# Three identity products between score products and row products in the gather loop of a graph-attention kernel

## The reference

```python
xn = _layernorm(x)
h = xn @ W_layer.T + b_layer
a1, a2 = h @ w_a1.T + b_a1, h @ w_a2.T + b_a2
v = leaky_relu(a1[row] + a2[col], 0.01)        # one score for each edge
ev = exp(v - segment_max(v, row)[row])
att = ev / segment_sum(ev, row)[row]
gnn = segment_sum(att[:, None] * h[col], row)  # the weighted rows, summed by target
x = x + gnn + mix(xn)                          # mix: the linear-attention branch
x = x + experts(_layernorm(x))                 # top 2 of 8, hidden width 682
```

## Time and profile before

| what | value |
|---|---|
| median of 3 runs | 2865.88 us |
| profiled execution | 2872.26 us |
| its span, first to last instruction | 2870.5 us |
| the gather, about | 440 to 1794 us of the span |
| PE busy, of the span | 2320.9 us (81%) |
| DVE busy, of the span | 1806.3 us (63%) |
| POOL busy, of the span | 1144.3 us (40%) |
| granted TensorE clock, mean of the span | 0.842 of full speed |

### The profile page before, as it was taken

One profiled execution on the slowest core, in us unless ns is written; L12 is line 12 of the kernel. 1 busy time (PEld: TensorE's weight loads), 2 busy tenths in 40 slices (PEclk: granted clock), 3 DMA queues, 4 the chain that ended last, 5 costly groups with the idle time before them and its releaser, 6 DMA issues.

```text
span 2870.5 us, 47292 instructions
## 1 busy us (share of the span) xinstructions
PE 2320.9 (81%) x12659; PEld 1906.3 (66%) x12683; DVE 1806.3 (63%) x6119; ACT 1253.3 (44%) x3758; POOL 1144.3 (40%) x1155
## 2 busy tenths in 40 slices
PE   3999984777877787778777878754599999999998
PEld 1677653555655565556555656643599999999997
DVE  8667763776777767777776667645355555555553
ACT  7444424555555555555555555432122222222222
POOL 0000005666666666666666663245222112112211
PEclk9999985788778777887788787765799999999999
DMA  2233213333333333333333335654122222222222
GB/s 71 92 115 99 90 59 85 88 89 89 89 89 89 89 89 89 89 88 89 90 89 89 89 88 52 213 179 157 52 36 36 34 36 35 36 34 36 36 35 28
DMA packets 127236, 226.62 MB, mean 79 GB/s; under 512 B 25553, under 2 KB 86482, under 8 KB 126214
## 3 DMA queue, kind: packets, MB, share of 16 engines
q0 software_dynamic: 62448, 142.98, 21.5%
q1 hardware_dynamic: 64534, 80.65, 9.0%
HBM read 169.81 MB, written 53.72 MB: 78 GB/s over the span
## 4 chain that ended last, share of the span: by engine, by line
PE 46%; DVE 18%; issue 16%; another core or an unknown queue 9%; DVEq 5%; POOL 2%; ACT 1%; DMA 1%; POOLq 0%; SPq 0%; ACTq 0%
PE psum L1614 18%; PE psum L1647 9%; PE psum L1102 6%; DVEq L1221 4%; DVE arena L1202 3%; PE psum L495 2%; DVE arena L824 2%; DVE arena L825 2%; DVE arena L1213 2%; PE psum L1353 1%; DVE arena L1246 1%; POOL expert_in L1574 1%; DVEq L1202 1%; PE psum L502 1%
## 5 line engine op out<-in xcount | busy, mean ns | idle before, releaser
L1075 POOL DMA_INDIRECT arena<-table,arena x880 | 864.2, 982 | 496.1 <-issue 235.9
L1102 PE MATMUL psum<-arena 128*128 128x257 f32 x1760 | 707.4, 540 | 293.6 <-DVE arena L1202 220.6
L1102 PEld LDWEIGHTS psum<-arena 128*128 128x128 f32 x1760 | 385.5, 255 | 509.3 <-issue 414.4
L1202 DVE SCALAR_TENSOR_TENSOR arena<-arena,psum 128x257 f32 x880 | 423.3, 481 | 358.8 <-remote 284.7
L1614 PE MATMUL psum<-arena 128*128 128x128 f32 x4620 | 552.1, 275 | 0.6 <-ACT arena L1669 0.6
L1614 PEld LDWEIGHTS psum<-arena 128*128 128x128 f32 x4620 | 542.5, 192 | 6.7 <-DVE arena L1711 0.9
L1751 POOL DMA_INDIRECT out<-arena x105 | 163.2, 1555 | 674.7 <-ACT arena L1676 664.6
L1129 ACT ACTIVATE arena<-arena 128x128 f32<-128x128 bf16 x880 | 281.2, 391 | 148.6 <-DVE arena L1216 108.4
L1647 PE MATMUL psum<-arena 128*128 x1260 | 290.5, 379 | 0.8 <-ACT arena L1676 0.8
L1142 ACT ACTIVATE arena<-arena 128x128 f32<-128x128 bf16 x880 | 281.2, 391 | 7.8 <-PE psum L1102 0.7
L1093 PEld LDWEIGHTS psum<-arena 128*128 128x128 f32 x1760 | 251.2, 220 | 19.1 <-issue 18.9
(11 more groups left out here) (332 smaller groups left out, 3093.1 us busy)
## 6 DMA issues: line engine op xcount, KB each, us to landing
arena<-table,arena POOLq DMA_INDIRECT x880
arena<-expert_in SPq DMA_DIRECT2D x105, 129.0 KB
mix_inputs<-arena SPq DMA_DIRECT2D x98, 128.0 KB
arena<-mix_inputs SPq DMA_DIRECT2D x49, 256.0 KB
arena<-in_w SPq DMA_DIRECT2D x6, 1364.0 KB
out<-arena SPq DMA_DIRECT2D x50, 128.0 KB
table<-arena SPq DMA_DIRECT2D x49, 129.0 KB
arena<-in_x SPq DMA_DIRECT2D x49, 128.0 KB, 3.6
```

The lines of the kernel that those rows point to most:

```text
L1075: pool.indirect_dma_start(rows_in[j][:, q * TW:(q + 1) * TW], None, table_d[:, :], bass.IndirectOffsetOnAxis(ap=col_all[:, t:t + 1], axis=0))\
L1102: mm(psum[4 + q][:, 0:C + 1], weight[b][:, q * P:(q + 1) * P], rows_in[g][:, q * TW:q * TW + C + 1], start=True, stop=True).then_inc(S("pr ...
L1202: v.scalar_tensor_tensor(here, here, alpha[(j - 5) % RING][:, q:q + 1], psum[4 + q][:, 0:C + 1], ALU.mult, ALU.add).then_inc(S("acc_done"), 1)
```

## The change

In each TensorE step that has score products, three more products are issued right behind the four score products and ahead of the four row products. Each multiplies the 128x128 identity matrix by itself, in float32, and writes 128 columns of PSUM bank i modulo 2. Nothing reads them: the transposes of the same step overwrite these columns. They carry no wait and no count, and `edge_done` is counted by the last score product, ahead of them.

```diff
@@ -53,6 +53,7 @@
 SLOPE = 0.01
+IDLE_GATHER = 3
 EPS = 1e-5
@@ -1093,6 +1094,8 @@
                         last = mm(psum[2 + b][:, 2 * q:2 * q + 2], member[b][:, q * P:(q + 1) * P], lb[b][:, q:q + G + 2:G + 1],
                                   start=True, stop=True)
                     last.then_inc(S("edge_done"), 1)
+                    for _ in range(IDLE_GATHER):
+                        mm(psum[b][:, 0:P], ident[:, :], ident[:, :], start=True, stop=True)
```

## The result

The change takes 2897.28 us (median of 4 runs, 2893.54 to 2899.50) beside 2863.07 us before (4 runs, 2858.85 to 2868.88): ratio 1.0117, 95% interval 1.0093 to 1.0140. It is slower by 34 us. The profiled execution of the change took 2895.72 us, its span is 2894.0 us, 23.5 us more than the span before.

What follows compares the result with a forecast made beforehand. The gather was taken as bound by waits on POOL's fetches, transfers and late-seen counts: 0 for 101 double steps, +2 for the end, 2865.9 + 2 = 2868 us; 2860 to 2876 if it holds, 8 in 10 for 2840 to 2905.

Steps and rivals of the forecast that it cites:

- TensorE as the bound at the lower clock: Slower rival, gather: low-clock double steps become TensorE-bound, 14.5 against 12.05 us; +15, +50 or +125 us; chance 0.27.
- What bounds the gather: Gather: a loop of POOL's eight fetches, their transfers and when product counts are seen sets 12.05 us, not TensorE's speed.
- double step: Gather: 12.05 us holding about two steps, eight POOL fetches and one wait each of POOL and DVE; 101 in 1217 us.
- The end of the gather: From 1775.45 us TensorE's own chain has no cover: two sets cost 1.4 to 2.6 us; taken as +2.
- The length of a set: Three added products in a gather step, six records: 0.72 us at the higher clock, 1.28 at the lower.
- The clock: Gather: denser TensorE work probably raises its granted clock somewhat; expected sign 0.78 or above.
- I cost this at nothing: Gather's 101 double steps: added TensorE work costs 0 us, covered by DVE's idle time and POOL's wait.
- The signs that the prediction named: Gather: 12.05 us double steps, 101 DVE waits of 2.8 us and POOL waits of 2.0 us, clock at least 0.78.
- Its last sign: The prediction fails if the late release of the counts in the gather hangs on TensorE's density; no size given.
- The faster rival: Gather: added products shift or break the late sight of counts; 10 to 30 us less, bound 2662 us; chance 0.19.

Runs made afterwards that it cites:

- free chip: Label for runs in which the kernel before takes 2594 to 2614 us; its profiled run there, without any edit, took 2608.15 us.
- held one: Held chip: label for runs in which the kernel before takes 2831 to 2869 us; the first measurement had 2863.07 us before.
- first chip: First measurement of the change, three products a step, against the kernel before: 2897.28 beside 2863.07 us, ratio 1.0117.
- second chip: Repeat of the unedited change against the kernel before, where that takes 2838.69 us: 2856.22 us, ratio 1.0058.
- e5_three: The change itself again, three products a step, no edit, against the kernel before: 2856.22 beside 2838.69 us, ratio 1.0058.
- e6_before_again: The kernel before, unedited, run once for its profile where the counts are not held back: 2608.15 us.

## Where the prediction was right and where it was wrong, point by point

The forecast was no change, 2868 us, and 2860 to 2876 us if its mechanism held; measured is 2897, +1.2%. That the time lies in the wide range of 2840 to 2905 us is luck: the range had been widened upward for TensorE as the bound at the lower clock, and that is not what came.

*What bounds the gather.* Right for the chip of the profile: the double step hangs on the fetches and on when counts are seen, and not on TensorE's speed. The free chip shows the same program without these waits. The prediction took the late counts for a property of the kernel; they depend on the chip or the moment too (0.014 or 0.015 us behind their products on the free chip, up to 4.4 us on the held one).

*The end of the gather.* Forecast +2 us, measured +1.2 between the two profiles; how much of it is cost and how much the clock's gain was not separated.

*The length of a set.* Forecast 0.72 us at the higher clock and 1.28 at the lower. On the chain at the end of the gather after, two sets stand like this:

```profile
1780.73 0.78 PE psum L1098 x6
...
1789.42 1.49 PE psum L1098 x6
```

The price at the higher clock was nearly right (0.78 us, at a granted clock of 1.00). That at the lower was too small: it took the record of a transpose (0.213 us) for that of a product, and the six records of a set take 1.49 us, at a granted clock of 0.50. No term of the sum for the double steps rests on it, since that was 0 either way.

*The clock.* Forecast 0.78 or above, measured 0.88. The rival "TensorE becomes the bound at the lower clock" had it at or under 0.72 and double steps of 13 us, and falls, though slower was right. One of its signs did come on the first chip: POOL waiting for L1105, 76.8 us in 44 pauses. The gather's clock was 0.88 with three products, and 0.97 with six on a held chip, and the higher clock brought nothing, as rows 6 had said.

*"I cost this at nothing."* This is the step that failed: the sum's 0 for the 101 double steps. Measured are +20.2 us in steps 24 to 215 on the first chip and +11.4 us on the second. It had three parts. That the fetches set the release: right. That TensorE's idle time before the release can be filled: only in part, since TensorE itself stopped in front of the added products (64 times 0.7 us on the first chip, 165 times on the second). Such a stop, in front of the row products, is in the kernel before too (63.2 us), and the prediction did not ask for it. On a free chip the same cover held for twice the amount (six products, ratio 1.0006 and 0.9985). That the release does not move: wrong. It moved by 0.12 to 0.18 us a double step. Read from the trace's record of the counts, medians over the double steps: POOL's last fetch of eight starts, and the last transfer begins 2.43 us later before and 2.44 after, but the first count of TensorE is seen 2.56 us later before and 2.69 after (92 and 76 double steps). The fetches are as quick as they were; TensorE's counts come through 0.13 us later behind them. For the run with products at the start only and for the change, both where the kernel before takes 2839 us, it is 2.42 and 2.50 us, with the last transfer at 2.43 and 2.44 (97 double steps each): 0.08 us, the same way. The signs that the prediction named did not tell this apart: on the second chip DVE still waited 98 times 2.8 us and POOL 98 times 2.0 us. Its last sign did, that it fails if the late release hangs on TensorE's density; the sum had no price for it. Rows 6 could not show this, because both of their stretches have the same instructions: they exclude a cost of TensorE's time, not one of more instructions.

*The start.* The prediction had no term for it. The stop of the fourth step was visible before, the trace has it, and I looked at the steady part and the end. Measured are +8.8 us in the two profiles and +6 us (interval +1 to +11) in the experiment that adds products only there. Whether the longer stop comes from the products of steps 2 and 3 themselves or from a chance that they shift is open; it was long (18.0 to 21.4 us) in all profiles with added products on held chips, and 10.8 us in the one without, and that is one profile.

*The faster rival.* It said that three products could shift how TensorE's work falls beside the fetches, and gave it a gain. The mechanism was near, the sign the other way. The held chips show no slower operand or transfer: in 540:1500 of the kernel before, DVE's add took 0.481 us on the held chip and 0.480 on the free one, and a packet of the fetches 0.164 us and 0.166 (30669 packets in 32.8% of the 16 DMA engines' 960 us, 36552 in 39.6%). But TensorE's counts, and then its issue, wait for the fetches to pause. In the double step of rows 5 the last fetch starts at 1008.07 us and the five counts come at 1010.66 to 1010.87; in the double step of the change shown above, the last starts at 1006.60, and the second set of added products at 1009.15, after 0.60 us of standing still.

Open: what makes a chip one of the held kind, and whether it is the chip at all; why TensorE's counts come later by 0.08 to 0.13 us when it has more to issue; why the loop changes to pauses after four fetches with six products, and now and then with three; whether three products cost nothing on a free chip, as one and six do; and whether instructions, columns or the clock carry the loss. For the last the narrow products ran twice, on free chips both times. That the release moved is measured; why it moved is not shown.

## What to carry to other kernels

Fill an engine's idle time only after asking what ends that idle time. Where TensorE's own counts were already waiting to be seen, up to 4.4 us in the kernel before, three products cost 34 and 17 us; where they were seen after 0.014 us, six cost none. A comparison inside one trace (two clocks, one program) frees you from one cause only, the one that differs. And where a wait has no releaser in the profile, run the kernel before on another chip, or at another time, first: here that was worth 255 us, seven times the change.

## What the runs showed of the hardware

- The same program took 2594 to 2614 us in some batches of runs and 2831 to 2869 us in others, and one chip number of the record stands beside both. In the slower kind 73% of TensorE's recorded semaphore counts stand more than 0.03 us behind the end of their products, up to 4.4 us, where all 1140 are 0.014 or 0.015 us behind it in the faster (the kernel before, 540:1500). They come in a burst, some 0.05 us apart (1010.66 to 1011.02 us in the double step of rows 5), when POOL's indirect fetches, one per 1.25 us, pause. ACT's recorded counts are not late there (all within 0.01 us), and of DVE's 92% are not.
- TensorE's issue stops as well: in the slower kind it stood still in front of the added products, which have no wait, 109.9 us in 1200 (`e5_three`), and in front of the row products 63.2 us in 1217 in the kernel before. In the faster kind the profile of the kernel before has no such stop of TensorE among its waits of 540:1500 (`e6_before_again`).
- On the free kind, with six added products a step (1320 in the gather), the clock was 1.00 over 960 us, where it was 0.88 without them, and the time the same within what the runs can tell (ratio 1.0006 and 0.9985).
